# ScalarE's copy of the embedding parts with three gather buffers, later loads on SyncE, and stops in VectorE's chains of one-hots

## The reference, cut to what matters

```python
# layer 0: sum of neighbours, scaled by degrees
msgs = label_mat[row] * norm[:, None]
x = _layernorm(x + segment_sum(msgs, col))
# layer 1: a gate for each edge
gate = silu(edge_attr @ W1.T + b1) @ W2.T + b2
ei, ej = emb[atom_z[src]], emb[atom_z[dst]]
gate = gate + sum(ei * (ej @ adaptW.T), axis=-1)
msg = gate * h[dst] * (cw * mj)[:, None]
agg = segment_sum(msg, src) / clip(segment_sum(mj, src), 1e-8)
x = layernorm(h + agg) * gamma + beta          # and one more normalization
```

## Time and profile before

| what | value |
|---|---|
| median of three runs | 3003.29 us (2993.86 to 3005.81) |
| the profiled execution's own time | 2972.2 us |
| its span | 2970.4 us |
| granted TensorE clock, mean | 0.858 |
| busy share PE, PEld, DVE, ACT, POOL | 75%, 64%, 80%, 47%, 71% |
| gathers (L718): count, busy, mean | 1616, 1793.1 us, 1110 ns |
| last gather starts, last scatter starts | 2668.70 us, 2757.27 us |

### The profile page before, as it was taken

The page is one execution under the profiler, slowest core; times in us unless marked ns, Lnnn a source line. Parts: engine busy times, 40 slices in busy tenths (PEclk is TensorE's granted clock), DMA queues, the critical chain, the costliest instruction groups (busy, mean ns, idle before and its releaser), DMA issues.

```text
span 2970.4 us, 73383 instructions
## 1 busy us (share of the span) xinstructions
PE 2221.1 (75%) x25909; PEld 1901.2 (64%) x25909; DVE 2378.4 (80%) x5426; ACT 1392.0 (47%) x2928; POOL 2098.4 (71%) x1852
## 2 busy tenths in 40 slices
PE   5980477778777877877787878777787877779675
PEld 5760356667666766766666667666666666667665
DVE  9994477777777777778788878878788888888798
ACT  7982244444444444444444444444444444445123
POOL 7506777777777777777777777777777777770255
PEclk9775688888888888888898888989889888889897
DMA  8405233344434334434355545545454554453895
GB/s 310 168 0 165 64 100 115 114 126 119 128 114 118 115 117 116 129 115 119 110 152 149 151 144 152 157 144 150 146 147 147 157 147 149 134 148 115 355 392 213
DMA packets 167497, 438.95 MB, mean 148 GB/s; under 512 B 85302, under 2 KB 85302, under 8 KB 147446
## 3 DMA queue, kind: packets, MB, share of 16 engines
q1 hardware_dynamic: 96266, 233.49, 23.7%
q0 software_dynamic: 67888, 194.98, 22.4%
q10 hardware_dynamic: 3004, 5.90, 0.6%
HBM read 291.23 MB, written 142.99 MB: 146 GB/s over the span
## 4 chain that ended last, share of the span: by engine, by line
POOL 46%; issue 17%; PE 16%; DMA 5%; DVE 5%; ACT 1%; POOLq 0%; SPq 0%; DVEq 0%; ACTq 0%
POOL slot L718 44%; PE acc L1593 4%; DMA slot<-table,gidx 3%; PE pwin L771 3%; PE phid L741 3%; PE route L815 2%; POOL slots L726 2%; PE pwin L850 2%; PE gate L753 2%; DVE oh_r L1083 1%; DMA oh_t<-dst_row 1%; DMA erows<-slots 0%; PE pwin L836 0%; DMA gidx<-src_pid 0%; DVE val L1201 0%
## 5 line engine op out<-in xcount | busy, mean ns | idle before, releaser
L718 POOL DMA_INDIRECT slot<-table,gidx x1616 | 1793.1, 1110 | 620.6 <-issue 606.9
L815 PEld LDWEIGHTS route<-parts,oh_r 128*128 128x128 bf16 x11312 | 773.4, 100 | 85.1 <-issue 60.9
L815 PE MATMUL route<-parts,oh_r 128*128 128x148 bf16 x11312 | 821.7, 233 | 3.3 <-DVE parts L1221 3.0
L1083 DVE TENSOR_SCALAR oh_r<-iota_r,spot 128x896 bf16<-128x896 f16 x1616 | 606.1, 445 | 70.9 <-PE route L815 70.9
L888 ACT ACTIVATE routed<-route 128x444 bf16<-128x444 f32 (+1 forms) x1010 | 508.8, 514 | 266.1 <-PE route L815 254.4
L850 PE MATMUL pwin<-slot,oh_d 128*128 128x144 bf16 x1616 | 177.0, 286 | 425.6 <-DMA slot<-table,gidx 393.3
L850 PEld LDWEIGHTS pwin<-slot,oh_d 128*128 128x128 bf16 x1616 | 156.1, 157 | 449.6 <-issue 319.8
L771 PEld LDWEIGHTS pwin<-win,oh_t 128*128 128x128 bf16 x4848 | 244.7, 111 | 139.1 <-issue 92.7
L741 PE MATMUL phid<-attr,w 80*96 80x512 f32 x404 | 278.8, 780 | 47.0 <-issue 46.4
L1187 DVE TENSOR_TENSOR prod<-slot,got 128x256 f32<-128x256 f32 x202 | 84.2, 417 | 260.0 <-ACT parts L949 259.9
L771 PE MATMUL pwin<-win,oh_t 128*128 128x80 bf16 (+1 forms) x4848 | 258.7, 218 | 18.1 <-ACT ssum L898 15.1
(11 more groups left out here) (227 smaller groups left out, 3314.7 us busy)
## 6 DMA issues: line engine op xcount, KB each, us to landing
rows<-slots SPq DMA_DIRECT2D x51, 1295.0 KB, 8.6
oh_t<-dst_row SPq DMA_DIRECT2D x101, 512.0 KB
erows<-slots SPq DMA_DIRECT2D x51, 777.0 KB
attr<-in_edge_attr SPq DMA_DIRECT2D x101, 320.0 KB
slots<-zeros SPq DMA_DIRECT2D x53, 518.0 KB
slot<-table,gidx POOLq DMA_INDIRECT x1616
table<-tab SPq DMA_DIRECT2D x3, 676.0 KB, 5.5
weight_t<-weights SPq DMA_DIRECT2D x101, 8.0 KB
```

Source lines behind the costliest of these rows:

```text
L718: e.indirect_dma_start(out=slot[:, s, g, :], out_offset=None, in_=table0, in_offset=bass.IndirectOffsetOnAxis(ap=gidx[:, s, g:g + 1], axis ...
L815: mm = e.matmul(route[:, (NPH * m + phase) % 2, RC * (j - a):RC * (j - a + 1)], oh_r[:, c, slot_of, :], parts[:, s % 2, c, :], start=(c == ...
L1083: oh = e.tensor_scalar(oh_r[:, c], iota_r[:, :, :], spot[:, s % 2, c:c + 1], None, ALU.is_equal)
```

## The change

Three parts, all in the tile stage.

1. `slot` has three buffers instead of six. A new ScalarE step `keep_emb` (lag 1, right behind `take_sums`) copies the embedding columns of a tile, 128 x 512 float32, into `kept`, which has six buffers; the logits read `kept`. A gather now waits for `summed` and for `emb_kept` of the tile three back.
2. SyncE's `load`, `rows` and `weigh` go from lag 4 to 7, `early_rows` from 5 to 8. `index` stays at 0.
3. In `route_onehots`, a wait ahead of each chain and one in its middle. Ahead of the chain of m = 0 it waits for `ohb` of t + 1, ahead of that of m = 1 for `split_ok` of 3t + 2; after four of the eight instructions the fourth increments `ohr`, and VectorE waits for that. TensorE's `routes` waits for the doubled count.

```diff
-            slot = sb("slot", [P, U, G, EX], F32, ph)
+            slot = sb("slot", [P, U // 2, G, EX], F32, ph)
+            kept = sb("kept", [P, U, G, EM], F32, ph)
...
-                    over_tiles(e, NT, U, (index, 0), (load, 4), (rows, 4), (weigh, 4),
-                               (early_rows, 5, EARLY_FROM))
+                    over_tiles(e, NT, U, (index, 0), (load, 7), (rows, 7), (weigh, 7),
+                               (early_rows, 8, EARLY_FROM))
...
-                    if since(i, s, U):
-                        e.wait_ge(summed, t - U + 1)
-                        e.wait_ge(gate_used, 2 * (t - U + 1))
+                    if since(i, s, U // 2):
+                        e.wait_ge(summed, t - U // 2 + 1)
+                        e.wait_ge(emb_kept, t - U // 2 + 1)
...
-                        e.wait_ge(ohr, 2 * t + m + 1)
+                        e.wait_ge(ohr, 2 * (2 * t + m + 1))
...
+                def keep_emb(i, s):
+                    t = U * i + s
+                    if since(i, s, U):
+                        e.wait_ge(gate_used, 2 * (t - U + 1))
+                    e.activation(kept[:, s], slot[:, s % (U // 2), :, 0:EM], ACT.Copy).then_inc(emb_kept, 1)
...
-                    over_tiles(e, NT, U, (take_sums, 1), (silu(0), 4), (put_got(0), 4), (put_got(1), 4), (silu(1), 4),
+                    over_tiles(e, NT, U, (take_sums, 1), (keep_emb, 1), (silu(0), 4), (put_got(0), 4), (put_got(1), 4), (silu(1), 4),
...
-                        for c in range(HC * m, HC * (m + 1)):
-                            oh = e.tensor_scalar(oh_r[:, c], iota_r[:, :, :], spot[:, s % 2, c:c + 1], None,
-                                                 ALU.is_equal)
-                        oh.then_inc(ohr, 1)
+                        if m == 0:
+                            e.wait_ge(ohb, t + 1)
+                        else:
+                            e.wait_ge(split_ok, 3 * t + 2)
+                        for half in range(2):
+                            for c in range(HC * m + HC // 2 * half, HC * m + HC // 2 * (half + 1)):
+                                oh = e.tensor_scalar(oh_r[:, c], iota_r[:, :, :], spot[:, s % 2, c:c + 1], None,
+                                                     ALU.is_equal)
+                            oh.then_inc(ohr, 1)
+                            if half == 0:
+                                e.wait_ge(ohr, 2 * (2 * t + m) + 1)
...
-                        e.tensor_tensor(prod[:, :, :], slot[:, s, m * HC:(m + 1) * HC, 0:EM],
+                        e.tensor_tensor(prod[:, :, :], kept[:, s, m * HC:(m + 1) * HC, :],
```

More of the change, by code:

```diff
@@ L623, in tile_programs @@
                                      "mid", "split_ok", "stepped", "group_rows", "ones_ok"))
-            erows_in, ecopied, emade, esummed = (
-                sem(n) for n in ("erows_in", "ecopied", "emade", "esummed"))
+            erows_in, ecopied, emade, esummed, emb_kept = (
+                sem(n) for n in ("erows_in", "ecopied", "emade", "esummed", "emb_kept"))
             (dst_at, all_at, v, a_own, w_ready, w_turned, w_out, rest_ok, weighed, query_r) = (
@@ L717, in gather @@
                     for g in range(G):
-                        e.indirect_dma_start(out=slot[:, s, g, :], out_offset=None, in_=table0,
+                        e.indirect_dma_start(out=slot[:, s % (U // 2), g, :], out_offset=None, in_=table0,
                                              in_offset=bass.IndirectOffsetOnAxis(ap=gidx[:, s, g:g + 1], axis=0)
@@ L847, in total @@
                         e.wait_ge(got_ok, 2 * (t - 3))
-                    rows = slot[:, s, :, EM:EX].bitcast(BF16)
+                    rows = slot[:, s % (U // 2), :, EM:EX].bitcast(BF16)
                     for g in range(G):
```

## The result

The changed kernel took 2953.21 us in the median of four runs (2950.96 to 2955.32), the kernel before 3001.03 us in four runs beside it (2993.86 to 3005.81). The ratio is 0.9853, with a 95% interval from 0.9828 to 0.9879: faster by 1.5%. The forecast was 2941 us with a range from 2885 to 3000.

A forecast was written before the change was run, and what follows sets the result against it. The prediction took POOL's gathers as the bound, with 3.6 us a tile to spare on the other engines. Its terms, -10.7 + 2 - 27.5 - 26 = -62 us, took 3003.3 us to 2941 us, range 2885 to 3000.

The forecast's parts named there:

- The total: Whole kernel: a gain of 62 us, the profiled execution's change standing for that of the other runs; 2941 us.
- Terms 3 and 4: POOL's gathers beside VectorE's one-hot chains: the stops save 27.5 us at m = 0 and 26 us at m = 1.
- Rival 1: One-hot chains: the stops free nothing, only the index waits go; 2995 us, chance 0.15.
- rival 2: One-hot chains: four short half chains block gathers as one long one did; slower, 3092 us, chance 0.12.
- Rival 3: One-hot chains: their whole cost to the gathers goes; 2852 us, chance 0.11 for more than 100 us gained.
- Term 2: VectorE's three stops a turn cost 0.15 us each, hidden except in the drain: +2 us.
- Term 1: SyncE's later loads let the index go out earlier, ending POOL's waits for indices: -10.7 us.
- slack hides it: Tile stage: the other engines' 3.6 us a turn to spare hide the copy (0.6 us) and the stops (0.45 us).
- Rival 4: Tile stage: the copy or the late loads make another engine the bound; chance under 2 in 100.
- The drain: Stretch behind the last gather: 88.6 us before, 88 to 92 us expected, with 2 us added by the stops.
- The copy and the buffers: ScalarE's copy takes about 0.61 us, 101 times, hidden; three gather buffers cost zero, POOL not waiting for `kept`.
- The rule of the Trainium skill: Shared port of VectorE and POOL: lock held for one instruction, so a wait of at most 0.445 + 0.115 us.

The follow-up runs named there:

- stops_only2: The kernel before with the stops in the one-hot chains alone, on a chip where the kernel before takes 2985.21 us: 2941.14 us, ratio 0.9861.
- no_stops2: The changed kernel without its stops, on the chip where the kernel before takes 2985.21 us: 2982.72 us, ratio 0.9997 to the kernel before.
- half_gathers: The changed kernel with every second gather left out: 2774.51 us, ratio 0.9293 to the kernel before (2985.21 us).
- no_stops: The changed kernel without its stops, on a chip where the kernel before takes 4134.89 us: 4439.8 us, ratio 1.075 to the kernel before.
- ahead_only: The changed kernel with a real stop ahead of both chains and none in the middle: 4338.0 us, ratio 1.0529 to the kernel before (4134.89 us).
- shift_only: The kernel before with SyncE's loads three turns later alone: 4432.07 us, ratio 1.0704 to the kernel before (4141.78 us).
- stops_only: The kernel before with the stops alone, on a chip where the kernel before takes 4141.78 us: 4244.73 us, ratio 1.0239.
- copy_only: The kernel before with three gather buffers and the copy alone: 4163.9 us, ratio 1.0062 to the kernel before (4141.78 us).

## Why the prediction was right or wrong

**The total.** The forecast was a gain of 62 us. The runs show 48 us (3001.03 to 2953.21). Those of stops_only2 (2985.21 to 2941.14) give 44 us for the stops alone. The prediction took the change of the profiled execution for that of the others. That isn't borne out: the two traces differ by 17 us, because the traced execution of the kernel before was a fast one (2972.2 us for a median of 3001). What follows explains the 17 us in full. Where the other 31 us of the medians lie, no trace shows.

**Terms 3 and 4, the stops: right in mechanism, near in size.** They stood at 27.5 + 26 = 53.5 us of POOL's time. The gathers' busy time fell by 59.5 us, the mean from 1110 to 1073 ns (1075 expected), the longest beside a chain to 2.39 us (2.4 expected). With the stops alone it fell by 36 us. What each half chain does to a gather stands in the timeline of the changed kernel around one first-half chain:

```profile
1275.68 0.57 DVE L1053 TENSOR_TENSOR oh_b<-number,bkt 128x816 bf16<-128x816 bf16 x1
...
1276.18 3.28 DVE L1095 TENSOR_SCALAR oh_r<-iota_r,spot 128x896 bf16<-128x896 f16 x8
1276.30 2.22 POOL L719 DMA_INDIRECT slot<-table,gidx  x1 [0.30 <-issue]
...
1278.82 1.09 POOL L719 DMA_INDIRECT slot<-table,gidx  x1 [0.30 <-issue]
```

The chain still begins before the buckets' one-hots end, so ahead of m = 0 the wait is no stop, as expected. The gather that begins 0.12 us into the chain takes 2.22 us, where one that began so early took 2.9 to 3.7 before, and the one behind it 1.09. It is let in at the stop in the middle. That is so for every held gather: 27 in the changed kernel and 31 in stops_only2 last 1.9 to 2.4 us, and all 58 end 0.81 to 0.83 us behind the end of the fourth one-hot. In the kernel before, 14 of the 22 end 0.82 to 0.86 us behind the eighth, and the other 8 only 0.12 us behind it, which the prediction didn't see. With the stops alone nearly all of the measured gain is there, without them none: 0.9861 against 0.9997. That is shown. Rival 1 (the stops free nothing) is out. So is rival 2 (four short chains block like one long one): the first half chains of m = 0 do hold a gather for their length, 27 of 101, but no other half chain does. Rival 3 (the whole cost of the chains goes) is out too: gathers still run over 0.945 us by 0.89 us at each first-half chain with no gap ahead (1.29 before), and by 0.34 at each second-half chain (0.56 before).

**Term 2, the price of a stop: within its bounds.** Assumed 0.15 us between bounds of 0.08 and 0.32. The second-half chain below takes 3.12 us, 0.14 more than before, and the gap ahead of it is 0.04 us (1495.65 + 0.55 = 1496.20, start at 1496.24) where before there were 0.08 of overlap, 0.12 us. That is a stop by itself. In the mean over all tiles a first-half chain takes 0.23 us more than before (3.02 to 3.25) and a second-half one 0.29 more (2.98 to 3.27), because some of VectorE's own one-hots last longer where POOL is let in (all of them 463 ns in the mean, 445 before). With the 0.12 us ahead of m = 1 this is 0.63 us a turn, in place of the 0.45 assumed.

```profile
1495.65 0.55 DVE L1235 TENSOR_TENSOR parts<-val,parts 128x384 bf16<-128x384 f32 x1
1496.24 3.12 DVE L1095 TENSOR_SCALAR oh_r<-iota_r,spot 128x896 bf16<-128x896 f16 x8
```

**Term 1, the indices: the wait went, no gain can be measured.** No wait for indices is left, as expected, and the term was priced at all its 10.7 us. no_stops2 takes this wait away too and gains nothing in its timed runs. POOL's own account in the traces, from the first gather to the last, shows where it went (us; the last row is the drain):

| | before | no_stops2 | stops_only2 | changed |
|---|---|---|---|---|
| first to last gather | 2429.4 | 2426.0 | 2391.7 | 2387.0 |
| gathers | 1791.8 | 1797.2 | 1755.8 | 1732.7 |
| scatters | 106.2 | 107.8 | 104.6 | 99.0 |
| waits for indices, over 0.3 us each | 10.7 | 0 | 9.1 | 0 |
| waits for ScalarE, over 0.3 us each | 0 | 0 | 0 | 32.4 |
| all other pauses | 520.8 | 520.9 | 522.1 | 522.8 |
| last gather to last scatter | 88.6 | 89.1 | 91.1 | 111.5 |

In no_stops2 the part behind the first gather of tile 51 did become 10.0 us shorter (1220.0 to 1210.0), so there the index waits had been on POOL's path. The part before it became 6.6 us longer, all of it in longer gathers. Whether that comes from the copy or from chance between two executions stays open.

**The step that failed: "slack hides it".** The 3.6 us a turn were worked out as TensorE's waits for gathers over the whole stage, 338.6 us over 95 tiles, and used everywhere: to hide the stops and the copy, and to count each microsecond of POOL's in full. In the changed kernel they didn't hide it: from 1846.9 us on POOL waits for ScalarE, 32.4 us up to the last gather, and the drain is 22.9 us longer. half_gathers measures the slack of the changed kernel: 2.7 us a turn up to tile 50, none behind. TensorE's wait for gathers behind tile 50 has turned into one for ScalarE. For the kernel before, 1475 to 2640 us, and then for the changed one in the same window:

```profile
PE pwin L850 <- DMA slot<-table,gidx: 158.1, 44, 5.9
```

```profile
PE pwin L772 <- ACT ssum L899: 127.9, 43, 4.4
...
ACT emine L982 <- DMA erows<-slots: 42.1, 33, 5.3
```

The loop that ends last in the changed kernel from some way behind tile 51 on runs from the early sum through the load of `erows`, ScalarE, VectorE and back to TensorE. It can't be seen as a wait for gathers. Rival 4 (the copy or the late loads make another engine the bound) was given under 2 in 100, because it was priced against the average of the stage. That another engine becomes the bound is what happened in the second half. What made it so isn't separated:

- Neither the stops alone (stops_only2) nor the copy and the later loads alone (no_stops2) do it. In both, POOL waits for no other engine up to its last gather, only for indices in stops_only2.
- In both, tiles 51 to 100 take less than the 24.6 us of the changed kernel: 24.16 us in stops_only2 and 24.30 in no_stops2. So the other engines of the kernel before, which have no stops to pay, could do with 24.2 us there, 0.3 under its 24.51. How much more slack they had isn't measured.
- The granted clock is a rival to the copy and the loads. In tiles 51 to 100 it was 0.89 before and in stops_only2, 0.90 in no_stops2, and 0.86 in the changed kernel, whose four timed runs all had a mean of 0.836 to 0.842. A matmul of TensorE's pick (L772 above) takes 0.270 us in the median there, 0.201 in the kernel before and in stops_only2 (1475 to 2455 us). The runs don't separate the clock's share.

So that the total of 48 us lies inside the range is in part luck: in the traces the gathers saved more than forecast (59.5 us for 53.5), and the other engines took back more than half of what POOL saved.

**The drain.** 88 to 92 us were expected, from two or three stops a turn. It is 111.5; with the stops alone it is 91.1. Once the gathers run ahead of engines that are the bound, what is saved ahead of the last gather comes back behind it: 40.5 us earlier, of which 22.9 are given back, 17.6 left at the last scatter (2739.71 for 2757.27). The average of the stage hid this as well.

**The copy and the buffers.** `kept` takes 0.621 us (0.61 expected), 98 times in the stretch, and POOL waits for it 0.6 us in all:

```profile
L906 ACT ACTIVATE kept<-slot 128x512 f32<-128x512 f32 x98 | 60.9, 621 | 0.0
```

**The rule of the Trainium skill.** The Trainium skill ("SBUF — State Buffer", section "SBUF: two separate sides") has the lock of the shared port held for one instruction. no_stops2 and the kernel before, with gathers of over 3.4 us beside instructions of 0.445 us each, disagree with it for instructions that follow each other without a gap. So do the gathers of up to 2.39 us that four one-hots hold in the kernels with stops; the real stop lets them in. The short delay until the loser gets in, about 115 ns by the Trainium skill, isn't contradicted: the held scatters of no_stops and 8 of the 22 gathers ended 0.12 us behind the chain.

## What to carry to other kernels

An engine's wait for the bottleneck is slack only if nothing else becomes its last wait, and only in the stretch in which it was read: where a stage changes its work half way (here the early sums from tile 51), read turn lengths and waits for each part, and price a saving by part. The cheapest test of how much an engine's speed-up can bring is to leave half of its work out and time the rest; it measures the kernel it is made in, at the clock it ran at. A long chain of VectorE's short instructions with no gap can shut POOL out for the whole of it; one wait for the instruction just ahead cost VectorE 0.12 us by itself, up to 0.3 us with what POOL then took, and ended that.

## What the runs showed of the hardware

- POOL's indirect DMAs, 0.94 us alone, take up to 3.7 us beside eight one-hots of VectorE that follow each other without a gap, and up to 2.39 us where a stop stands in the middle. A held gather ends 0.81 to 0.86 us behind the last one-hot without a gap, or 0.12 us behind it. Over the kernel this is 1.4% (0.9861 [0.9833, 0.9889]).
- Scatters are held too, 2.60 to 2.62 us in place of some 1.0, at 15 of the 100 second-half chains that one meets in no_stops and at none in ahead_only.
- The same kernel takes 2985 us on one chip and 4135 to 4147 us on others. On the slower ones turns of tiles 11 to 50 take 36.1 to 37.2 us whichever edits a kernel has (23 to 24 elsewhere). ScalarE then waits, mostly 2.5 to 8 us at a time, for something the profile calls remote, and TensorE waits for ScalarE. This falls mostly where POOL issues a burst of gathers: between 600 and 3900 us ScalarE is busy 0.17 to 0.26 of the time in a burst (POOL's instructions less than 1 us apart) and 0.48 to 0.50 between bursts. The median gather takes the same 0.94 us. The first gather starts at 241 to 243 us in seven of the nine runs, as elsewhere, and at 280 and 282 us in shift_only and stops_only. With the loads early (copy_only, stops_only) a turn of tiles 51 to 100 takes 35.6 and 36.6 us, with the later loads 39.5 to 41.0. What these waits are for stays open.
